# Second edge loop of a graph network: target one-hots built by ScalarE and VectorE, the direct product by GpSimd, counts fetched block by block

## The reference, cut to what matters

```
hs_e, hv_e = hs[src], hv[src]            # node features of the source: 8 scalars, 8 vectors of 3
m0 = ALPHA * (einsum('eu,euw->ew', hs_e * sh0, W00) + INV_SQRT3 * einsum('eui,ei,euw->ew', hv_e, sh1, W110))
m1 = ALPHA * (einsum('eu,ei,euw->ewi', hs_e, sh1, W01) + einsum('eui,euw->ewi', hv_e * sh0, W10))
messages = concatenate([m0, m1])
agg = segment_sum(messages, dst)         # 3125 x 32
```

## Time and profile before

| | |
|---|---|
| median of three runs | 3043.38 us |
| the profiled execution's own time | 3040.35 us |
| its span, first to last instruction | 3037.9 us |
| mean granted TensorE clock, share of full speed | 0.853 |
| busy over the span: PE, DVE, ACT, POOL | 78%, 65%, 32%, 48% |
| the second edge loop | about 1777 to 2424 us |

### The profile page before, as it was taken

The page is one execution under the profiler, slowest core; times in us unless marked ns, Lnnn a source line. Parts: engine busy times, 40 slices in busy tenths (PEclk is TensorE's granted clock), DMA queues, the critical chain, the costliest instruction groups (busy, mean ns, idle before and its releaser), DMA issues. The chain is left out here.

```text
span 3037.9 us, 72809 instructions
## 1 busy us (share of the span) xinstructions
PE 2359.2 (78%) x27993; PEld 1700.1 (56%) x27993; DVE 1976.0 (65%) x5117; ACT 965.9 (32%) x1879; POOL 1470.1 (48%) x1845
## 2 busy tenths in 40 slices
PE   0538877999159999999999735888888759996696
PEld 0213333333038888888888523555555549995574
DVE  5815444444179999999999635999899835443001
ACT  1014333333015555555555312444344300000010
POOL 2017777777515555555555225999899800000000
PEclk9957666555569999999999857999999969997897
DMA  8954444444203333334334267555555330003955
GB/s 358 367 221 115 114 113 113 114 113 111 78 19 110 110 126 137 110 116 147 110 109 153 92 155 183 144 150 147 145 145 150 97 77 3 3 3 123 419 242 244
DMA packets 251426, 424.06 MB, mean 140 GB/s; under 512 B 127586, under 2 KB 213244, under 8 KB 241747
## 3 DMA queue, kind: packets, MB, share of 16 engines
q1 hardware_dynamic: 195124, 334.25, 31.4%
q0 software_dynamic: 54800, 83.75, 11.0%
q10 hardware_dynamic: 1164, 1.37, 0.1%
HBM read 229.60 MB, written 209.72 MB: 145 GB/s over the span
## 5 line engine op out<-in xcount | busy, mean ns | idle before, releaser
L331 POOL DMA_INDIRECT sorted_edges<-s_records,s_index x400 | 476.3, 1191 | 312.8 <-issue 308.3
L1529 PE MATMUL m_p_acc<-m_prod,m_oh 128*128 128x344 f32 x1250 | 412.2, 474 | 17.7 <-issue 17.3
L1083 DVE TENSOR_SCALAR e_ohw<-e_iota,e_rec 128x128 bf16<-128x128 f32 x628 | 400.2, 696 | 0.0
L867 POOL TENSOR_TENSOR e_ohw<-e_oh,e_rec 128x512 bf16<-128x512 bf16 x314 | 332.3, 1078 | 76.0 <-DVE e_oh L1075 76.0
L1529 PEld LDWEIGHTS m_p_acc<-m_prod,m_oh 128*128 128x128 f32 x1250 | 232.9, 196 | 121.4 <-issue 31.5
L873 POOL TENSOR_TENSOR e_part<-e_rest,e_part 128x256 bf16<-128x256 f32 x157 | 103.7, 660 | 401.1 <-ACT e_part L903 395.1
L1432 POOL TENSOR_SCALAR m_oh<-m_iota,m_rec 128x128 f32<-128x128 f32 x314 | 264.4, 852 | 0.1
L1786 PE MATMUL q_p_next<-q_g,A 128*128 128x96 bf16 x5250 | 224.8, 206 | 0.0
L1786 PEld LDWEIGHTS q_p_next<-q_g,A 128*128 128x128 bf16 x5250 | 223.7, 98 | 0.0
L1097 DVE COPY e_strip<-e_p_aw 128x512 f32<-128x512 f32 (+1 forms) x325 | 199.9, 656 | 1.4 <-PE e_p_aw L975 1.2
L1576 DVE TENSOR_TENSOR m_prod<-m_rec,m_coef 128x256 f32<-128x256 f32 x471 | 198.4, 472 | 0.0
(11 more groups left out here) (346 smaller groups left out, 4883.8 us busy)
## 6 DMA issues: line engine op xcount, KB each, us to landing
dense_strips<-e_strip SPq DMA_DIRECT2D x25, 3200.0 KB, 11.1
r_W<-dense_strips SPq DMA_DIRECT2D x47, 1600.0 KB, 24.7
m_rec<-sorted_edges SPq DMA_DIRECT2D x138, 526.0 KB, 3.8
sorted_edges<-s_neg SPq DMA_DIRECT2D x5, 12560.0 KB, 68.2
A<-dense_strips POOLq DMA_DIRECT2D x25, 800.0 KB, 24.4
e_rec<-sorted_edges SPq DMA_DIRECT2D x156, 108.0 KB, 2.2
sorted_edges<-s_records,s_index POOLq DMA_INDIRECT x400, 3.9
m_rec<-sorted_edges SPq DMA_DIRECT2D x12, 394.5 KB, 3.4
```

What stands on the lines that cost most here:

```text
L331: pool.indirect_dma_start(dram["edges"], bass.IndirectOffsetOnAxis(ap=index[u % RING][:, c:c + 1], axis=0), record[u % RING][:, c, :], Non ...
L867: i = g_.tensor_tensor(ohw[g % 4][:, :, k, :], oh[s][:, :, 0, :], rec[s][:, :, c:c + 1].to_broadcast([P, G, P]), ALU.mult)
L1083: i = V.tensor_scalar(ohw[g % 4][:, t, 0, :], iota[:, :], rec[s][:, t, CSRC:CSRC + 1], rec[s][:, t, CW:CW + 1], ALU.is_equal, ALU.mult)
L1529: i = mm(p_acc[d % 2][:, 0:TERMS], oh[g % 4][:, t % G, :], prod[g % 3][:, t % G, :], start=(t % NB == 0), stop=(t % NB == NB - 1), skip_gr ...
```

## The change

Target one-hots of tiles 0 to 2 of each group are made by ACT: three Squares of 128 columns, d = (target - column)^2, into a new buffer `away`, and one Relu of 1 - d over 384 columns. DVE makes only tile 3's. POOL makes none; instead it computes the direct product, which DVE did. SP's loads wait on ACT's offsets and DVE's sum instead of POOL's one-hots. The 18 blocks of counts are fetched one every eighth step of POOL from step 0 on, instead of all at step -4.

```diff
+        AHT = 3
+        away = ring("away", [P, AHT, P], 2)
@@ sync
-                onehots.before(sp, g, SLOTS)
+                offset.before(sp, g, SLOTS)
+                summed1.before(sp, g, SLOTS)
@@ gpsimd
-            def one_hots(g):
-                s = g % SLOTS
-                pool.wait_ge(loaded[s], arrivals[g])
-                sum_done.before(pool, g, 4)
-                pool.sem_inc(prime, 1)
-                for t in range(HALF_G):
-                    i = g_.tensor_scalar(oh[g % 4][:, t, :], iota[:, :], rec[s][:, t, RDST:RDST + 1], None, ALU.is_equal)
-                onehots.set_by(i)
+            def direct_products(g):
+                pool.wait_ge(loaded[g % SLOTS], arrivals[g])
+                summed1.before(pool, g, 2)
+                directed.set_by(g_.tensor_tensor(direct[g % 2][:, :, :, :], rec[g % SLOTS][:, :, RT + 2 * MM:RT + 3 * MM]
+                                                 .rearrange("p t (w u) -> p t w u", w=MUL),
+                                                 node[g % 4][:, :, SS:SD].unsqueeze(2).to_broadcast([P, G, MUL, MUL]), ALU.mult))
-                staged(j, (dot_products, 4), (scale, 4), (dot_sum, 4), (one_hots, 2), (dot_total, 4))
-                if j == -4:
-                    bring_counts(pool, dram, keep["A"], range(EARLY))
+                staged(j, (dot_products, 4), (scale, 4), (dot_sum, 4), (direct_products, 4), (dot_total, 4))
+                if j >= 0 and j % 8 == 0 and j // 8 < EARLY:
+                    bring_counts(pool, dram, keep["A"], range(j // 8, j // 8 + 1))
@@ scalar
+            def target_offsets(g):
+                s = g % SLOTS
+                act.wait_ge(loaded[s], arrivals[g])
+                onehots.before(act, g, 2)
+                for t in range(AHT):
+                    i = nc.scalar.activation(away[g % 2][:, t, :], iota[:, :], ACT.Square, bias=rec[s][:, t, RDST:RDST + 1], scale=-1.0)
+                offset.set_by(i)
+
+            def target_one_hots(g):
+                offset.after(act, g)
+                sum_done.before(act, g, 4)
+                onehots.set_by(nc.scalar.activation(oh[g % 4][:, 0:AHT, :], away[g % 2][:, :, :], ACT.Relu, bias=one[:, :], scale=-1.0))
-                staged(j, (square, 6), (node_copy, 5), (one_hot, 6))
+                staged(j, (square, 6), (target_offsets, 3), (node_copy, 5), (one_hot, 6), (target_one_hots, 3))
@@ vector
-            def direct_products(g):
...
             def direct_sums(g):
                 directed.after(dve, g)
+                made_outer.before(dve, g, 2)
...
-                wide = [P, G - HALF_G, P]
+                wide = [P, G - AHT, P]
...
-                staged(j, (scalar_products, 3), (direct_products, 3), (vector_products, 3), (direct_sums, 3), (one_hots, 3), (outer_products, 3),
+                staged(j, (scalar_products, 3), (vector_products, 3), (direct_sums, 3), (one_hots, 3), (outer_products, 3),
                        (finish, 0))
```

More of the change, by code:

```diff
@@ L32 @@
 G = 4
-HALF_G = G // 2
 NG = -(-NB * NB // G)
@@ L1365, in layer1_edges_phase @@
         dotted, dot_added, scaled, made_coef = (step(name) for name in ("dotted", "dot_added", "scaled", "made_coef"))
+        offset = step("offset")
         onehots, onehots2, directed, summed1 = (step(name) for name in ("onehots", "onehots2", "directed", "summed1"))
@@ L1566, in scalar_products @@
                                 coef[g % 3][:, :, SS:SE].unsqueeze(2).to_broadcast([P, G, MUL, 2 * MUL]), ALU.mult)
-            def direct_products(g):
-                directed.set_by(V.tensor_tensor(direct[g % 2][:, :, :, :], rec[g % SLOTS][:, :, RT + 2 * MM:RT + 3 * MM]
-                                                .rearrange("p t (w u) -> p t w u", w=MUL),
-                                                node[g % 4][:, :, SS:SD].unsqueeze(2).to_broadcast([P, G, MUL, MUL]), ALU.mult))
             def vector_products(g):
@@ L1587, in one_hots @@
                 sum_done.before(dve, g, 4)
-                wide = [P, G - HALF_G, P]
-                onehots2.set_by(V.tensor_tensor(oh[g % 4][:, HALF_G:G, :], iota[:, :].unsqueeze(1).to_broadcast(wide),
-                                                rec[s][:, HALF_G:G, RDST:RDST + 1].to_broadcast(wide), ALU.is_equal))
+                wide = [P, G - AHT, P]
+                onehots2.set_by(V.tensor_tensor(oh[g % 4][:, AHT:G, :], iota[:, :].unsqueeze(1).to_broadcast(wide),
+                                                rec[s][:, AHT:G, RDST:RDST + 1].to_broadcast(wide), ALU.is_equal))
             def outer_products(g):
```

## The result

The changed kernel takes 2968.62 us (median of four runs, 2966.53 to 2972.49) against 3043.02: ratio 0.976, 95% interval 0.9735 to 0.9785. 74 us are gained where 112 were forecast. The profiled execution's span is 2966.7 us, 71.2 less; the second edge loop is 74.3 shorter and the rest 3 longer.

What follows compares the result with a forecast made beforehand. Held to be bound by the ring of record slots, no engine being full. Gain 135.3 us from start and step, less 18 for blocks and 5 for slow steps: 112 off 3040.35, median 2931; range 2886 to 2976, 2992 with part of Rival (1).

Steps and rivals of the forecast that it cites:

- The ring: Second edge loop: six record slots, each held until POOL's one-hots end, 22.13 us a round, 3.69 per group.
- Its removal brings the step to 3.2: Second edge loop: once record slots no longer bind, the step falls from 3.73 to 3.2 us, bounds 3.05 and 3.5.
- What is late next is PE: Second edge loop after the change: PE binds, floor 3.05 us, with ACT at 3.0 and DVE at 2.8 close behind.
- V: DVE's step per group after the change: 2.38 us undisturbed, taken as 2.7 beside POOL, at most 3.05.
- The start: Loop's beginning: without the crowd of blocks, spread(6) starts near 1790.4 us instead of 1816.99, spread(7) at 1795.9.
- A block costs 1.0 us, 18 in all: Counts fetched within the loop: 3.96 us delay per block less slack leaves 1.0, 18 us in all, bounds 0 and 71.
- 5 us kept for slow steps: Second edge loop: allowance of 5 us for a few steps that lose to the clock.
- waits of 4 at each block: Sign of a wrong forecast: waits of 4 us at each block of counts in the loop.
- The slack of 2.6 to 3.4: Record slots after the change: round of 15.8 us against 19.2 for six steps, 3.4 us spare, 2.6 at step 3.05.
- Rival (1): Each of 18 blocks of counts stalls PE for its full 3.96 us, 71 instead of 18: 2984 us, chance 0.06.
- The direct product on POOL, 0.65 with a stretch: POOL's added 128x256 product per group: 0.65 us plus a stretch by DVE, bounds 0.63 and 1.60.
- Rival (2): DVE's two-input products and POOL's products exclude each other in the loop: step 3.96 us, total 3026, chance 0.08.

Runs made afterwards that it cites:

- e6: Old kernel with eight slots of records instead of six, nothing else changed: 2995.3 us, ratio 0.987.
- e1: Changed kernel with all 18 blocks of counts fetched after the second edge loop instead of within it: 2977.2 us, ratio 0.9792.
- e3: Changed kernel with the fetch put back as before, all 18 blocks at POOL's step -4: 2969.1 us, ratio 0.9759.
- e7: Changed kernel with eight slots of records instead of six, whole blocks of counts every eighth group: 2918.9 us, ratio 0.9618.
- e10: Changed kernel with eight slots, the direct product back on VectorE and the one-hots of all four tiles on ScalarE: 2895.5 us, ratio 0.9516.
- e8: Changed kernel with eight slots and each block fetched in four quarters, one every second group: 2943.3 us, ratio 0.9686.
- e9: Changed kernel with eight slots and the direct product put back on VectorE: 2901.3 us, ratio 0.9534.

## Why the prediction was right, and where its sum was off

- *The ring bound the old loop, and POOL's one-hots held the slot*: right, shown by e6. *Its removal brings the step to 3.2*: right as a number, 3.20 in e1 and 3.23 in e3.
- *What is late next is PE*: wrong. PE's floor of 2.89 to 3.05 was read right (2.89 in the profile after), but DVE is full at 3.20. The step that failed is V, 2.7 by the forecast and 3.10 measured. The undisturbed 2.38 fits: with POOL idle from 2070.46 on, DVE's step of 2069.68 to 2072.10 took 2.42. So the stretch by GpSimd's products is about 0.7 and not 0.3. That 3.2 came out as the number is luck: it was the margin that I put on PE's floor.
- *The start*: right. spread(6) 13.4 us after spread(0) (forecast 12.6, before 39.2), spread(7) 16.2 after it (forecast 18.1); the clock rose within the first sums.
- *A block costs 1.0 us, 18 in all*: this is the term that was mis-sized. It costs 3.4, 62 in all; with 5 us kept for slow steps the sum is off by 39, and that is the whole gap between 112 and 74. About 0.7 of the 3.4 is no stall, since e7, which has none, steps in 3.29 where e1 steps in 3.20; the forecast gave POOL's issues a cost of nothing. The delay of at most 4 us per block was about right, and PE's waits of 3.2 on average come near the waits of 4 at each block that the forecast had named as a sign against it. The slack of 2.6 to 3.4 was not there: V was too short, and between two blocks PE steps in 2.89 while DVE needs 3.2, so DVE falls behind by 0.3 per group (it starts group 89 0.18 us after its coefficients, group 94 2.55 after) and hands its slots back later each time. The load for the spread at 2063.61 was issued at 2059.71, 3.9 us ahead: the ring stood at its limit when the block came. Rival (1), which I gave 0.06, is nearly what happened, and the clock's drop behind each wait is part of its price.
- *The direct product on POOL, 0.65 with a stretch*: 0.69 where undisturbed, 0.81 on average. Rival (2) had the mechanism at a chance of 0.08, but not the size: the move of this product loses 0.13 us per group where the rival has the step at 3.96. *ScalarE at 2.7 to 3.0*: 417.06/470 of 3.20 is 2.84, right; it became the bound only with a fourth tile (e10).

The forecast of the sign and the range held, with the median near the slow end of 2886 to 2976. The two parts of the gain, the start and the step, came from where they were said to come, but the blocks gave back as much as the start had gained: by e3 the net gain is that of the new split of work alone. The step that a reader should distrust is a slack worked out with undisturbed durations.

## What to carry to other kernels

Where several engines are all 85 to 90% busy, follow one slot of the ring around before moving work: here two more slots in the old kernel gave 42 us, and eight slots with the fetch spread gave as much as the whole change did. Moving a two-input product from VectorE to GpSimd saved 0.33 us and cost 0.46 on VectorE itself; the one-hots that went to ScalarE held nothing up as long as it had room (2.84 of 3.20 us in e1). Spread a bulk transfer in pieces whose delay is less than the ring's slack, in no more issues than that takes (e8), and take that slack from the slowest engine's measured step, not from PE's.

## What the runs showed of the hardware

- A block of counts (800 KB, on GpSimd's queue) in flight does not share the DMA engines evenly with a record load: q0 held 92.9% and q1 0.2% from 2063 to 2067 us, with a load issued at 2063.39, and the load took 7.0 us instead of 3.8.
- In the changed kernel each of PE's waits for a block-delayed load from 1830 us on, 2.1 to 4.4 us long, was followed by a step at a granted clock of 0.50 to 0.68. The wait of 4.19 (sums of 4.73 us instead of 2.53 behind it) made two steps of 7.29 and 5.25 instead of 2.89 each, so it delayed PE by 6.8.
- An issue of such a transfer by GpSimd, recorded as 0.58 us, lengthened the step of a full VectorE by about 0.5 us, in e8 with quarters as in e7 and e9 with whole blocks (0.7 and 1.0 per block). Why is open.
